# Attention plus conditioned feed-forward on one core: every second unit's two weight addends go to TensorE, products two units behind, rings of six

## The chip, the cores and the metric

One core of one Trainium2 chip runs the whole program. The metric is device time in microseconds (us), the median of several executions. TensorE (PE) multiplies, VectorE (DVE), ScalarE (ACT) and GpSimd (POOL) do element work, SyncE (SP) issues the transfers.

## The reference, cut to what matters

```python
x = x + attn(cond(x, ids, W, b), w_qkv, w_out, slopes)        # x: (2, 2048, 512) fp32
x = x + ffn_int8(cond2(x, ids2, W1, b1, W2, b2, gamma, beta), w8, w8_scale, bias)
# attn, 16 heads of 32:
scores = q @ k.T * scale + alibi;  scores = where(causal, NEG, scores)
num = 0.5 * (1.0 + scores * rsqrt(1.0 + scores * scores))
out = (num / (num.sum(-1) + EPS)) @ v
# cond: x @ W[id] + b[id].   cond2: layer norm of (x + relu(x @ W1 + b1) @ W2 + b2), times gamma, plus beta
```

The kernel never forms `num` itself. With s a score, y = 1/sqrt(1 + s^2) and g = s*y it holds g^2 + y^2 = 1, so (1+g)^2 + y^2 = 2 (1+g) = 4 num. The weight that multiplies v is therefore the sum of two addends, (1+g)^2 and y^2. The factor 4 drops out against the denominator.

## The kernel before, in words

The main part is eight groups, four for each of two batches; a group is four heads. A group walks 40 **units**: a unit is a chunk `c` of 512 queries against a block `kb` of 128 keys, 4 (c+1) blocks for chunk c, so the chunks have 4, 8, 12 and 16 units. The last four units of a chunk lie on the causal diagonal and are 512, 384, 256 and 128 queries wide. A unit is two **pairs** k = 2u and 2u+1 of two heads; a pair's tile is 128 x 1024 at full width. For each pair, in this order:

- PE writes the scores into one of two PSUM slots (L825; on the diagonal with a mask, L828), once the pair two before has given its slot free;
- ACT squares them into `yb` (L669), then takes 1/sqrt(1 + .) in place (L671): y;
- DVE multiplies scores by y into `gb` (L1042): g, which frees the slot;
- POOL squares y in place (L623); ACT makes (1+g)^2 in place (L661), two pairs later in its queue;
- DVE adds the two (`numerator`, L983), two pairs later;
- PE multiplies the sum with v into `ov` and with ones into `dn` (`products`, L804), four heads side by side in columns of 32. It stands `LAG` = 3 units behind the scores. `ov` and `dn` are one PSUM bank each: when a chunk is finished DVE copies both out (L996, L997; between groups L1078, L1079), and only then may the next chunk's first product start (`s_out`). Six and twelve pairs later come a reciprocal and `divide` (L1007).

Between the scores the PE does **parts** of other jobs: projections of q, k, v (`Group`, a planner that fills PE time after each pair's scores). Groups 1, 2, 5 and 6 are `plain` and have only their 12 projections. `opening` (group 0) and `closing` (group 3) also compute the conditioned input h (jobs `xt`, `h`). `joining` (group 4) and `ending` (group 7) also do the output projection and the adapter with its norm for the finished batch (jobs `o`, `rt`, `a`, `w2`, `zt`), 16 and 10 tiles; each job's PSUM result is emptied by DVE into SBUF, all counted by one semaphore `s_evac`. All engines walk the same list of events of a group, each taking its own part; every queue is in order. Plain groups run in hardware loops of two turns.

Of the kernel before, what the change touches and what calls it, by code (L numbers as in the profile page):

```python
# [7 lines left out]
ALU = mybir.AluOpType  # L8
ACT = mybir.ActivationFunctionType
# [14 lines left out]
NORMED = 2  # L24
STAGED = 3
YRING = 4
GRING = 8
NUM_LAG = 2
LAG = 3
# [51 lines left out]
def woven(jobs_of, tiles, n=2):  # L81

    return number([job for j in tiles[::n] for step in zip(*[jobs_of(j + i) for i in range(n)]) for job in step])


class Group:
# [4 lines left out]
    def __init__(self, n_chunks, others, has_next, opens=False, slack=0.0):  # L91
# [30 lines left out]
        for k in range(2 * len(self.units)):  # L122
# [24 lines left out]
            if k % 2:  # L147
                self.events.append(("pv", k // 2 - LAG))
# [4 lines left out]
        assert len(self.items) % BANKS == 0 or not has_next  # L153
# [10 lines left out]
def adaln_attn_ffn(nc, x, ids_cond, ids_lang, cond_w, cond_b, w_qkv, w_out, slopes, W1, b1, W2, b2,  # L164
# [35 lines left out]
    assert PAIRS % YRING == 0 and PAIRS % GRING == 0  # L200
# [6 lines left out]
    def runs(b):  # L207

        return [(0, opening if b == 0 else joining, 1), (1, plain, NG - 2), (NG - 1, ending if b == B - 1 else closing, 1)]

    starts, n = {}, PRO
    for b in range(B):
        for hg, g, count in runs(b):
            starts[b, hg] = n
            n += count * len(g.items)
    REST = n
    PRO_JOBS = woven(cond_jobs, range(TT))
    END_JOBS = woven(after_jobs, range(DONE, KB), KB - DONE)
    PLACES = 2 + KB - DONE
# [9 lines left out]
    def for_groups(eng, body):  # L229

        for b in range(B):
            for hg0, g, count in runs(b):
                if count == 1:
                    body(b, hg0, b * NG + hg0, g, starts[b, hg0])
                else:
                    with eng.Fori(hg0, hg0 + count) as hg:
                        body(b, hg, b * NG + hg, g, starts[b, hg0] - hg0 * len(g.items) + hg * len(g.items))

    with ExitStack() as ctx:
# [13 lines left out]
        yb = sb("yb", [P, YRING, 2 * CH])  # L253
        gb = sb("gb", [P, GRING, 2 * CH])
# [17 lines left out]
        rstd = sb("rstd", [P, PLACES])  # L272
        amax = sb("amax", [P, B * KB])
# [33 lines left out]
        s_evac = sem("s_evac")  # L307
        s_hi = sem("s_hi")
# [6 lines left out]
        s_g2 = sem("s_g2")  # L315
        s_num = sem("s_num")
# [37 lines left out]
        ring_y = yb[:, :, :].rearrange("p a n -> p (a n)")  # L354
        ring_g = gb[:, :, :].rearrange("p a n -> p (a n)")
# [8 lines left out]
        woT_s = gb[:, 0:2, :].rearrange("p a n -> p (a n)").rearrange("p (m c) -> p m c", m=KC)  # L364
        wqT_s = gb[:, 2:8, :].rearrange("p a n -> p (a n)").rearrange("p (g s k n) -> p g s k n", g=NG, s=3, k=KC)
        w8T_s = area[:, 2 * KC * C:2 * KC * C + KC * C // 2].bitcast(BF16).rearrange("p (m c) -> p m c", m=KC)
        idx = yb[0:64, 0:2, :].rearrange("p a n -> p (a n)").bitcast(I32)

        z0 = gb[:, :, :].rearrange("p (k a) n -> p k (a n)", k=KC)
        x10 = kst[:, :, :].bitcast(F32)  # L370
        zq = yb[:, :, :].rearrange("p a n -> p (a n)").bitcast(BF16).rearrange("p (a k n) -> p a k n", a=4, k=KC)
# [11 lines left out]
        def yview(k):  # L383
            return yb[:, k % YRING, :].rearrange("p (h n) -> p h n", h=2)

        def gview(k):
            return gb[:, k % GRING, :].rearrange("p (h n) -> p h n", h=2)

        def q0_of(g, k):

            return g.width(k // 2 % UNITS)
# [17 lines left out]
        def ops_before(g, G):  # L409

            return 2 if g is opening else 2 * NC * G + 3

        @block.sync
        def _(sp):
# [82 lines left out]
            def after(b, job, i):  # L497
# [4 lines left out]
                if what == "o":  # L502
                    sp.wait_ge(s_evac, i + 1)
# [3 lines left out]
                elif what == "zt":  # L507
# [3 lines left out]
                    sp.wait_ge(s_evac, i + 1)  # L511
                    sp.dma_start((hT if b == B - 1 else z_d)[:, :, tok], resT[a]).then_inc(s_zst[a], 16)

            def group(b, hg, G, g, base):
# [3 lines left out]
                if g in (joining, ending):  # L518
                    d = b if g is ending else b - 1

                    sp.wait_ge(s_evac, base)
# [3 lines left out]
                if g is closing:  # L525
                    sp.wait_ge(s_evac, base)
# [3 lines left out]
                for e in g.events:  # L530
# [9 lines left out]
                    what, c = e[1].name[0:2]  # L540
                    if what in ("q", "k"):
# [599 lines left out]
```

## Time and profile before

| | |
|---|---|
| time, median of 3 (lowest, highest) | 2264.09 us (2263.49, 2267.63) |
| the profiled execution | 2265.64 us, span 2263.8 us |
| mean granted PE clock | 0.907 of full |
| busy: DVE, PE, POOL, ACT | 1878.6, 1803.9, 1715.7, 1685.0 us |
| share of the span: DVE, PE, POOL, ACT | 83%, 80%, 76%, 74% |

Busy is the time in which an engine works on at least one instruction; overlapping ones count once. A PE that is busy at half clock does half as much. The shares are means over eight groups with different limits, so the groups have to be read one by one.

### The profile page before, as it was taken

Reading aid. Unit: us, or ns where it says so; the run is one execution under the profiler, and the core shown is the slowest. Engines: PE = TensorE matmul, PEld = TensorE weight load, DVE = VectorE, ACT = ScalarE, POOL = GpSimd, SP = SyncE. Lnnn points to the kernel's source line nnn. Section 1 sums busy time; section 2 is a strip of 40 time slices with the busy share of each in tenths; the row PEclk is TensorE's granted clock in tenths of the full one; section 3 lists DMA queues with packets and bytes.
Section 4 is the critical chain, followed back from the end, with each engine's and each line's share of the span. In section 5 each row is a group of like instructions: output and inputs, shape, how many; then the busy total and the mean of one; then the engine's idle time right before and its main releaser. Section 6 shows DMA issues by size and latency. Waiting matters only on the chain.

```text
span 2263.8 us, 31228 instructions
## 1 busy us (share of the span) xinstructions
PE 1803.9 (80%) x10640; PEld 904.5 (40%) x10640; DVE 1878.6 (83%) x2114; ACT 1685.0 (74%) x1938; POOL 1715.7 (76%) x784
## 2 busy tenths in 40 slices
PE   5678877877787789998888877877787787887864
PEld 4555323333333346664444433333333333342331
DVE  4358888888889888889789898888888888899768
ACT  0247897989889888889567667999889888767413
POOL 2136887788878887788678887788878887788548
PEclk9899988988898899999999998988988898998879
DMA  5411111110111022202322221110111021121137
GB/s 176 146 49 44 49 30 35 43 45 25 40 40 49 20 69 66 68 25 74 84 77 81 69 54 34 40 49 21 45 40 48 20 79 44 42 62 52 59 123 237
DMA packets 126620, 138.68 MB, mean 61 GB/s; under 512 B 27868, under 2 KB 78044, under 8 KB 126044
## 3 DMA queue, kind: packets, MB, share of 16 engines
q1 hardware_dynamic: 126460, 136.64, 21.5%
q8 instruction: 89, 1.46, 0.3%
q14 instruction: 71, 0.58, 0.1%
HBM read 54.02 MB, written 22.80 MB: 34 GB/s over the span
## 4 chain that ended last, share of the span: by engine, by line
PE 38%; ACT 21%; DVE 20%; issue 12%; POOL 4%; DMA 2%; SPq 2%; DVEq 0%; POOLq 0%; ACTq 0%
ACT yb L669 9%; PE sc L825 7%; PE ov L804 7%; ACT yb L671 7%; DVE gb L1042 6%; PE dn L804 6%; ACT gb L661 6%; DVE gb L983 5%; PE it L723 5%; PE it L740 4%; PE it L747 4%; PE it L727 3%; POOL oT L654 2%; SPq L428 2%; PE it L707 1%
## 5 line engine op out<-in xcount | busy, mean ns | idle before, releaser
L623 POOL TENSOR_TENSOR yb<-yb 128x1024 f32<-128x1024 f32 (+3 forms) x640 | 1510.2, 2373 | 460.9 <-DVE gb L1042 448.6
L669 ACT ACTIVATE yb<-sc 128x1024 f32<-128x1024 f32 (+3 forms) x640 | 566.9, 886 | 376.3 <-PE sc L825 189.8
L1042 DVE TENSOR_TENSOR gb<-sc,yb 128x1024 f32<-128x1024 f32 (+3 forms) x640 | 676.6, 1057 | 186.1 <-ACT yb L671 183.9
L983 DVE TENSOR_TENSOR gb<-gb,yb 128x1024 f32<-128x1024 f32 (+3 forms) x640 | 779.2, 1218 | 3.9 <-ACT gb L661 0.5
L825 PE MATMUL sc<-qmv,kst 128*128 128x512 f32 (+3 forms) x1280 | 505.6, 472 | 295.8 <-DVE gb L1042 278.2
L671 ACT ACTIVATE yb<-yb 128x1024 f32<-128x1024 f32 (+3 forms) x640 | 595.0, 930 | 20.3
L661 ACT ACTIVATE gb<-gb 128x1024 f32<-128x1024 f32 (+3 forms) x640 | 584.1, 913 | 0.1
L825 PEld LDWEIGHTS sc<-qmv,kst 128*128 128x128 f32 x1280 | 238.7, 209 | 648.3 <-DVE gb L1042 453.3
L804 PE MATMUL ov<-gb,vv 128*32 128x512 f32 (+3 forms) x2560 | 338.4, 604 | 18.0 <-DVE den L997 10.5
L804 PE MATMUL dn<-gb,ones 128*32 128x512 f32 (+3 forms) x2560 | 326.3, 584 | 0.0
L723 PE MATMUL it<-hT,wT 128*128 128x512 f32 x496 | 249.9, 629 | 5.8 <-DVE area L921 1.8
L804 PEld LDWEIGHTS dn<-gb,ones 128*32 128x32 f32 x2560 | 90.2, 121 | 181.9 <-issue 176.3
L740 PE MATMUL it<-area 128*128 128x128 f32 x1024 | 131.2, 284 | 19.4 <-DVE area L904 18.3
L740 PEld LDWEIGHTS it<-area 128*128 128x128 f32 x1024 | 126.4, 199 | 26.7 <-DVE area L904 21.8
L723 PEld LDWEIGHTS it<-hT,wT 128*128 128x128 f32 x496 | 97.8, 204 | 82.7 <-issue 66.5
L747 PE MATMUL it<-area,oT 128*128 128x512 f32 x224 | 116.3, 648 | 17.4 <-DVE oT L1007 5.7
L727 PE MATMUL it<-wT,hT 128*128 128x128 f32 x992 | 124.5, 279 | 2.9 <-DVE stage L901 2.3
L727 PEld LDWEIGHTS it<-wT,hT 128*128 128x128 f32 x992 | 121.1, 194 | 8.8 <-DVE stage L901 2.5
L828 PE MATMUL sc<-unseen,ident 128*128 128x128 bf16 x512 | 121.8, 243 | 0.0
L804 PEld LDWEIGHTS ov<-gb,vv 128*32 128x32 f32 x2560 | 52.4, 112 | 133.4 <-issue 82.2
L707 PE MATMUL it<-ident,area 128*128 128x128 f32 x336 | 53.5, 293 | 29.3 <-DMA area<-in_x_dram 13.1
L899 DVE TENSOR_SCALAR stage<-it 128x512 fp32r<-128x512 f32 x64 | 43.7, 683 | 34.7 <-PE it L723 20.8
(112 smaller groups left out, 1093.5 us busy)
## 6 DMA issues: line engine op xcount, KB each, us to landing
qmv<-stage SPq DMA_DIRECT2D x384, 64.0 KB
kst<-stage SPq DMA_DIRECT2D x384, 64.0 KB
area<-in_x_dram SPq DMA_DIRECT2D x58, 256.0 KB, 2.8
out_dram<-oT SPq DMA_DIRECT2D x32, 256.0 KB, 3.3
den<-rec_d SPq DMA_DIRECT2D x31, 256.0 KB
wT<-wT_d SPq DMA_DIRECT2D x7, 768.0 KB, 4.4
x_d<-area SPq DMA_DIRECT2D x16, 256.0 KB, 2.6
z_d<-area SPq DMA_DIRECT2D x16, 256.0 KB, 3.2
```

What stands on the lines that cost most here:

```text
L623: pool.tensor_tensor(y, y, y, ALU.mult).then_inc(s_y2, 1)
L661: act.activation(t, t, ACT.Square, bias=1.0).then_inc(s_g2, 1)
L669: act.activation(y, sc[:, k % SLOTS, :, q0_of(g, k):], ACT.Square).then_inc(s_s2, 1)
L671: act.activation(y, y, ACT.Abs_reciprocal_sqrt, bias=1.0).then_inc(s_y, 1)
L723: r = pe.matmul(bank, wT[:, "qk".index(what), part, :], hT[:, part, c * CH:(c + 1) * CH], **ends)
L727: r = pe.matmul(bank[:, part * P:(part + 1) * P], hT[:, k, tok], wT[:, 2, k, :], start=(k == 0), stop=(k == KC - 1))
L740: r = pe.matmul(bank[:, part * P:(part + 1) * P], wc[:, k, part * P:(part + 1) * P], xT[:, a, k, :], start=(k == 0), stop=(k == KC - 1))
L747: r = pe.matmul(bank, oT[:, part, tok], woT[:, part, :], **ends)
L804: r = pe.matmul(dst[h * D:(h + 1) * D, q0:], lhsT, gview(2 * u + h // 2)[:, h % 2, q0:], start=(kb == 0), stop=last_kb)
L825: r = pe.matmul(slot[:, i, q0:], kst[:, h, kb * P:(kb + 1) * P], qmv[:, c % 2, h, q0:], start=True, stop=not on_diagonal)
L983: dve.tensor_tensor(t, t, yview(k)[:, :, q0:], ALU.add).then_inc(s_num, 1)
L1042: dve.tensor_tensor(gview(k)[:, :, q0:], sc[:, k % SLOTS, :, q0:], yview(k)[:, :, q0:], ALU.mult).then_inc(s_g, 1)
```

## The change

1. Pairs get a kind by their number: `KINDS = ("split", "split", "sum", "sum")`. In even units (both pairs split) DVE makes no sum; PE accumulates (1+g)^2 and y^2 one after the other, 16 products in place of 8. In odd units all stays, with lags of one pair in place of two.
2. `LAG` 3 to 2 units, and the product is placed after the scores of an even pair instead of an odd one. The copy of a finished chunk is put off (`leaving`) until after the next odd pair's g.
3. Rings: y four and g eight tiles before, six and six now.
4. The PSUM results of `rt`, `a` and `zt` are emptied by ACT, with a count of their own (`s_evac_act`); the maximum over z stays on DVE (`largest`). The norm on POOL takes one more small instruction.
5. The loops over plain groups are written out.

```diff
-YRING = 4
-GRING = 8
-NUM_LAG = 2
-LAG = 3
+RING = 6
+KINDS = ("split", "split", "sum", "sum")
+SQUARE_LAG = 1
+SUM_LAG = 1
+LAG = 2
...
-            if k % 2:
+            if k % 2 == 0:
                 self.events.append(("pv", k // 2 - LAG))
...
             def products(G, g, u):
-                pe.wait_ge(s_num, G * PAIRS + 2 * u + 2)
+                n = G * PAIRS + 2 * u
+                for m in (n, n + 1):
+                    if kind(m) == "split":
+                        pe.wait_ge(s_y2, m + 1)
+                        pe.wait_ge(s_g2, squared(m) + 1)
+                    else:
+                        pe.wait_ge(s_num, summed(m) + 1)
                 last_kb = kb == TT * (c + 1) - 1
+                heads = [(h, gview(n + h // 2)[:, h % 2, q0:], True, kind(n + h // 2) != "split") for h in range(HG)]
+                heads += [(h, yview(n + h // 2)[:, h % 2, q0:], False, True) for h in range(HG) if kind(n + h // 2) == "split"]
                 for dst, is_v in ((ov, True), (dn, False)):
-                    for h in range(HG):
+                    for h, weights, begins, ends in heads:
...
                 def scored(k):
                     dve.tensor_tensor(gview(n)[:, :, q0:], sc[:, n % SLOTS, :, q0:], yview(n)[:, :, q0:],
                                       ALU.mult).then_inc(s_g, 1)
-                    if k >= NUM_LAG or carry:
-                        numerator(G, g, k - NUM_LAG)
+                    if n >= SUM_LAG and kind(n - SUM_LAG) != "split":
+                        numerator(n - SUM_LAG)
+                    while reduced and reduced[0][0] < k:
+                        largest(*reduced.pop(0)[1:])
+                    if k % 2 and leaving:
+                        u, c = leaving.pop()
+                        if u >= 0:
+                            output(G, hg, g, u, c, g is opening and c == 0)
+                        else:
+                            output_prev(G, prev_hg, u, c)
...
+            def after(b, job, item, z_before):
+                act.wait_ge(s_item, item + 1)
+                if what == "rt":
+                    act.activation(resT[a], feat, ACT.Copy).then_inc(s_evac_act, 1)
+                elif what == "a":
+                    act.activation(hid[a], bank[:, 0:P], ACT.Relu, bias=b1c[:, 0:1]).then_inc(s_evac_act, 1)
+                elif what == "zt":
+                    for k in range(KC):
+                        r = act.activation(resT[a][:, k, :], feat[:, k], ACT.Identity, scale=gam[:, k:k + 1],
+                                           bias=bet[:, k:k + 1])
```

How the queues stand in a plain group where the products pass from chunk 0 (units 0 to 3) to chunk 1 (from unit 4). On PE before: the scores of pair 14, two parts of a projection, the scores of pair 15, two parts, then the first product of unit 4, which waits for `s_out`.

```order
L825 MATMUL sc<-qmv,kst 128x512 [waits s_g]
L825 MATMUL sc<-qmv,kst 128x512
L833 REGISTER_ALU
L716 REGISTER_ALU [waits s_evac]
L723 MATMUL it<-hT,wT 128x512 [waits s_evac]
L723 MATMUL it<-hT,wT 128x512
L817 REGISTER_ALU
L825 MATMUL sc<-qmv,kst 128x512 [waits s_g]
L825 MATMUL sc<-qmv,kst 128x512
L723 MATMUL it<-hT,wT 128x512 x2
L847 REGISTER_ALU
L804 MATMUL ov<-gb,vv 32x512 [waits s_num,s_evac,s_out]
```

On PE in the changed kernel, the same passage: the last product of chunk 0 (unit 3, width 128), the scores of pair 11, two parts, the scores of pair 12, then unit 4's product.

```order
L902 MATMUL ov<-ring,vv 32x128 [waits s_num]
L902 MATMUL ov<-ring,vv 32x128 x3
L902 MATMUL dn<-ring,ones 32x128 x4
L924 MATMUL sc<-qmv,kst 128x512 [waits s_g]
L924 MATMUL sc<-qmv,kst 128x512
L816 MATMUL it<-hT,wT 128x512 x2
L924 MATMUL sc<-qmv,kst 128x512 [waits s_g]
L924 MATMUL sc<-qmv,kst 128x512
L902 MATMUL ov<-ring,vv 32x512 [waits s_g2,s_y2,s_evac,s_out]
L902 MATMUL ov<-ring,vv 32x512 x7
L902 MATMUL dn<-ring,ones 32x512 x8
L924 MATMUL sc<-qmv,kst 128x512 [waits s_g]
```

Unit 4's product moved from behind pair 15 to behind pair 12, has 16 matmuls in place of 8, and no part stands directly ahead of it any more.

On DVE before, the copy of chunk 0: the division of the chunk before, g of pair 13, a numerator, the copy and the denominator.

```order
L1007 TENSOR_TENSOR oT<-oT,den 128x512 [waits s_out]
L1041 REGISTER_ALU [waits s_pv]
L1042 TENSOR_TENSOR gb<-sc,yb 128x1024 [waits s_y]
L983 TENSOR_TENSOR gb<-gb,yb 128x1024 [waits s_g2,s_y2]
L992 REGISTER_ALU
L995 REGISTER_ALU [waits s_pv]
L996 ISA [waits s_norm]
L996 COPY oT<-ov 128x512
L997 TENSOR_SCALAR den<-dn 128x512
```

On DVE in the changed kernel, the same: g of pairs 9 and 10, the division, a projection's two instructions (`stage`), g of pair 11, the numerator of pair 10, the copy and the denominator.

```order
L1147 TENSOR_TENSOR ring<-sc,ring 128x1024 [waits s_y,s_pv] x2
L1109 TENSOR_TENSOR oT<-oT,den 128x512 [waits s_out,s_den]
L1002 TENSOR_SCALAR stage<-it 128x512 [waits s_op,s_qk,s_item]
L1004 SCALAR_TENSOR_TENSOR stage<-it,stage 128x512 [waits s_hi]
L1147 TENSOR_TENSOR ring<-sc,ring 128x1024 [waits s_y,s_pv]
L1085 TENSOR_TENSOR ring<-ring 128x1024 [waits s_g2,s_y2]
L1098 COPY oT<-ov 128x512 [waits s_norm,s_pv]
L1099 TENSOR_SCALAR den<-dn 128x512
```

The copy moved from behind g of pair 13 to behind g of pair 11, two pairs, while the product that waits for it moved three pairs.

## Rows read from the trace of the kernel before

**Rows 1.** Busy time by stretch; rows are groups 0, 1, 3, 4, 5, 7 and the tail
```profile
core 0: us, PE busy (x) PEld busy (x) DVE busy (x) ACT busy (x) POOL busy (x), PEclk, DMA share, GB/s
90.40:371.90 281.50, 227.56 (x1471) 131.73 (x1471) 209.62 (x215) 207.54 (x240) 190.36 (x80) 0.92 0.16 42
371.90:604.30 232.40, 181.29 (x1057) 79.56 (x1057) 198.74 (x197) 205.44 (x240) 191.86 (x81) 0.89 0.15 37
...
836.20:1075.60 239.40, 223.09 (x1633) 139.24 (x1632) 215.87 (x229) 206.80 (x241) 192.32 (x81) 0.99 0.21 59
1075.60:1392.60 317.00, 269.37 (x1473) 133.77 (x1472) 282.79 (x389) 209.74 (x241) 249.79 (x129) 0.96 0.25 68
1392.60:1624.20 231.60, 180.82 (x1057) 79.43 (x1057) 198.38 (x197) 205.41 (x240) 191.47 (x81) 0.89 0.15 38
...
1856.80:2138.20 281.40, 224.87 (x1220) 105.10 (x1222) 246.43 (x306) 205.89 (x238) 223.34 (x109) 0.88 0.18 49
2138.20:2263.80 125.60, 77.11 (x340) 34.86 (x332) 93.81 (x150) 32.54 (x22) 78.07 (x54) 0.87 0.56 180
```
**Rows 2.** Groups of ACT instructions in plain group 5 (1392.6 to 1624.2)
```profile
L669 ACT ACTIVATE yb<-sc 128x1024 f32<-128x1024 f32 x56 | 56.6, 1011 | 13.7 <-PE sc L825 9.2 <-PE sc L828 2.4 <-DVE gb L983 2.0
...
L671 ACT ACTIVATE yb<-yb 128x256 f32<-128x256 f32 x8 | 3.3, 417 | 0.3
```
**Rows 3.** Timeline where group 5 passes from chunk 0 to 1: start, duration, instruction
```profile
1473.24 1.00 ACT L669 ACTIVATE yb<-sc 128x1024 f32<-128x1024 f32 x1
...
1475.22 2.38 DVE L1007 TENSOR_TENSOR oT<-oT,den 128x512 f32 x1
...
1476.18 1.01 ACT L669 ACTIVATE yb<-sc 128x1024 f32<-128x1024 f32 x1
...
1477.22 1.06 ACT L671 ACTIVATE yb<-yb 128x1024 f32<-128x1024 f32 x1
1477.52 1.21 DVE L1042 TENSOR_TENSOR gb<-sc,yb 128x1024 f32<-128x1024 f32 x1
...
1478.65 1.21 DVE L983 TENSOR_TENSOR gb<-gb,yb 128x1024 f32<-128x1024 f32 x1
...
1479.36 1.88 PE L723 MATMUL it<-hT,wT 128*128 128x512 f32 x4
...
1479.79 0.68 DVE L996 COPY oT<-ov 128x512 f32 x1
...
1480.39 0.68 DVE L997 TENSOR_SCALAR den<-dn 128x512 f32<-128x512 f32 x1
...
1481.16 1.06 PE L804 MATMUL ov<-gb,vv 128*32 128x512 f32 x8
...
1482.05 1.04 PE L804 MATMUL dn<-gb,ones 128*32 128x512 f32 x8
...
1483.02 0.73 PE L825 MATMUL sc<-qmv,kst 128*128 128x512 f32 x2
1483.25 0.68 DVE L899 TENSOR_SCALAR stage<-it 128x512 fp32r<-128x512 f32 x1
...
1483.79 1.02 ACT L669 ACTIVATE yb<-sc 128x1024 f32<-128x1024 f32 x1 [0.75 <-PE sc L825]
1483.96 0.69 DVE L901 SCALAR_TENSOR_TENSOR stage<-it,stage 128x512 fp32r<-128x512 f32 x1
```
**Rows 4.** Timeline of PE in group 5 after a wait, clock granted at half
```profile
1410.55 1.93 PE L804 MATMUL ov<-gb,vv 128*32 128x512 f32 x8 [1.36 <-DVE den L1079]
...
1414.12 1.22 PE L825 MATMUL sc<-qmv,kst 128*128 128x512 f32 x2
```
**Rows 5.** PE's waits in group 7 (1856.8 to 2138.2): total us, times, longest
```profile
PE it L747 <- DVE oT L1007: 5.7, 1, 5.7
PE it L747 <- issue: 5.6, 1, 5.6
```
**Rows 6.** Timeline of DVE in group 7: one `zt` tile emptied
```profile
2014.64 1.36 DVE L930 TENSOR_SCALAR area<-it,gam,bet 128x128 f32<-128x128 f32 x4
```

More of the change, by code:

```diff
@@ L207, in runs @@
     def runs(b):
-        return [(0, opening if b == 0 else joining, 1), (1, plain, NG - 2), (NG - 1, ending if b == B - 1 else closing, 1)]
-    starts, n = {}, PRO
+        return ([(0, opening if b == 0 else joining)] + [(hg, plain) for hg in range(1, NG - 1)] +
+                [(NG - 1, ending if b == B - 1 else closing)])
+    starts, n = {}, (PRO, PRO, 0)
     for b in range(B):
-        for hg, g, count in runs(b):
+        for hg, g in runs(b):
             starts[b, hg] = n
-            n += count * len(g.items)
-    REST = n
+            n = tuple(v + w for v, w in zip(n, (len(g.items), g.evacs["dve"], g.evacs["act"])))
+    REST, REST_DVE, REST_ACT = n
     PRO_JOBS = woven(cond_jobs, range(TT))
     END_JOBS = woven(after_jobs, range(DONE, KB), KB - DONE)
+    END_ITEMS = [job for job in END_JOBS if job.parts]
+    END_RANKS, END_EVACS = ranks(END_ITEMS)
     PLACES = 2 + KB - DONE
@@ L227, in tiles_in, with for_groups @@
         return 1 if a >= 2 else (B * KB - (KB - DONE)) // 2
-    def for_groups(eng, body):
+    def for_groups(body):
         for b in range(B):
[L232 to L237, printed above, removed]
+            for hg, g in runs(b):
+                body(b, hg, b * NG + hg, g, starts[b, hg])
     with ExitStack() as ctx:
@@ L381, in adaln_attn_ffn, with kind, before, summed @@
         wq_t = w_qkv.rearrange("(s m p) c -> p s m c", s=3, p=P)
[L383 to L391, printed above, removed]
+        def kind(n):
+            return KINDS[n % len(KINDS)]
+        def before(n, *kinds):
+            count = [k in kinds for k in KINDS]
+            return n // len(KINDS) * sum(count) + sum(count[:n % len(KINDS)])
+        def summed(n):
+            return before(n, "fold", "sum")
+        def squared(n):
+            return before(n, "split", "sum")
+        def yview(n):
+            return ring[:, n % RING, :].rearrange("p (h n) -> p h n", h=2)
+        def gview(n):
+            return ring[:, RING + n % RING, :].rearrange("p (h n) -> p h n", h=2)
+        def q0_of(n):
+            return plain.width(n % PAIRS // 2)
         def div_steps(g, carry):
@@ L411, in ops_before, with zs_before @@
             return 2 if g is opening else 2 * NC * G + 3
+        def zs_before(b, j):
+            order = [job.name[1] for job in (ending if b == B - 1 else joining).items if job.name[0] == "zt"]
+            n = KB * b
+            return n + (order.index(j - 2) + 1 if j >= 2 else 0)
         @block.sync
@@ L553, in group @@
                     elif what in ("o", "zt"):
-                        after(b if g is ending else b - 1, e[1], base + item)
+                        after(b if g is ending else b - 1, e[1], base + item, (act_base if what == "zt" else dve_base) + rank)
                     item += 1
-            for_groups(sp, group)
+            for_groups(group)
             sp.wait_ge(s_pv, B * NG * UNITS)
@@ L675, in _ @@
             act.wait_ge(s_chain, 9)
             act.wait_ge(s_wst, 48)
[L677 to L679 removed]
+            for_groups(group)
+            for n in range(TOTAL - SQUARE_LAG, TOTAL):
+                if kind(n) != "fold":
+                    one_plus_g_squared(n)
+            for job, (eng, rank) in zip(END_ITEMS, END_RANKS):
+                if eng == "act":
+                    after(B - 1, job, REST + job.index, 0)
@@ L1079, in output_prev @@
                 dve.tensor_scalar(den[:, :], dn[:, :], SOFT_EPS, None, ALU.add).then_inc(s_out, 1)
-            for_groups(dve, group)
-            for k in range(-NUM_LAG, 0):
-                numerator(B * NG, plain, k)
+            for_groups(group)
+            for n in range(TOTAL - SUM_LAG, TOTAL):
+                if kind(n) != "split":
+                    numerator(n)
             output_prev(B * NG, NG - 1, -1, NC - 1)
```

273 lines of the change are left out of this document (165 added, 108 removed).

## The prediction

> **What bounds the kernel now.** DVE is the busiest engine of the whole, but the stages differ, so I cut the span where ACT squares the first pair of each group and read the busy times of each stretch [rows 1]. The reader is to see three kinds. A plain group takes 231.6 us and ACT works 205.4 of them, PE 180.8, DVE 198.4: ACT is the nearest to a limit. At full width its three passes over a pair come round in 2.94 us when nothing holds them (1473.24 to 1476.18) [rows 3]; its 26.2 us of idle time stand mostly before L669, for scores that PE brings late [rows 2]. In closing PE works 223.1 of 239.4 us at a clock of 0.99: PE bounds it. In joining DVE works 282.8 of 317.0 and PE 269.4: both. Opening and ending are mixtures, with PE at 227.6 of 281.5 and 224.9 of 281.4 [rows 1]. So a change that takes work from DVE and gives it to PE helps joining at best, and has to be paid in closing.
>
> **What is added to PE.** One product at full width and full clock takes from 1481.16 to 1483.02, 1.86 us: 0.89 for `ov`, 0.97 for `dn` with what lies before the next scores [rows 3]. The added addend repeats both: the doubled product takes 1.78 + 1.86 = 3.64 us. Of a group's 20 even units 16 are full and 4 are 256 wide; counting those as half, 18 x 1.78 = 32 us of PE time for each group. Less per group is not possible, as the four column groups are already used side by side.
>
> **What is taken from DVE.** In the half of the pairs that are split the L983 addition goes, 1.21 us each [rows 3], 36 full-width equivalents or 43 us a group. In joining DVE also loses 16 x (0.68 + 0.34 + 1.36) for `rt`, `a`, `zt`; the 1.36 is [rows 6], the 0.68 the COPY of [rows 3], 0.34 is a quarter of the 1.36. That is 38 us more: 283 falls to about 202. DVE stops being a limit anywhere. ACT gets those jobs: not less than 1.9 us a tile if it does them at its own speed per element, not more than 0.6 + 0.4 + 4 x 0.42 = 2.7 us if each 128-wide piece costs what 256 columns cost it [rows 2]. 16 tiles are 30 to 43 us on 209.7, far below the 301 us that PE needs there, so I cost it at nothing; if that cover were gone it would be those 30 to 43.
>
> **What moves: the passage from chunk to chunk.** This is the term I give most weight. `ov` and `dn` are single, so the next chunk's first product waits for DVE's copy. Before, that product stands behind the scores of pair 15, which themselves wait for g of pair 13, and the copy follows g of 13 and one numerator: the two come together, and ACT loses only 0.75 us (the row at 1483.79) [rows 3]. Now the product stands behind the scores of pair 12, which need only g of pair 10, while the copy stands behind g of 11 and the numerator of 10. Let T be the start of ACT's square of pair 11. g(11) starts at T + 2.08 (1.01 + 1.06 for the two passes); from the start of g to the start of the product rows 3 give 1481.16 - 1477.52 = 3.64 us (g, sum, copy, denominator). So the product starts at T + 5.72. It is unit 4, an even one, and doubled: the scores of pair 13 start at T + 9.36, ACT's square 0.77 later (1483.02 to 1483.79), at T + 10.13. ACT wanted it at T + 5.88. It stands still for 4.2 us. All four first units of a chunk (0, 4, 12, 24) are even, so all four passages have this form. In two of them a division and a projection's two evacuations stand ahead of that g: the division would start at T + 0.27 and, with 2.30 to the next (1475.22 to 1477.52) and 0.68 + 0.69, puts g at about T + 3.9 instead of T + 2.08: 6.0 us. The passage between groups, at narrow pairs, I take as the mean of these three, 5.4. Together 21.6 us for a group with nothing else in PE's queue there. The PE idles for some 5 us in each.
>
> **The plain group.** Floor 205.4; passages 21.6. Doubled products also follow two projection parts at four places: from the end of g, 0.09 + 0.57 for scores, 1.8 for parts, 3.64, 0.77 are 6.9 us against the 5.5 that ACT allows, 1.3 each; three more stand at 256-wide pairs, about 1 each: 8 us. A rest of 1. The clock: after a wait of 1.36 us in [rows 4] the granted clock was at half, and one product took 1410.55 to 1414.12, 3.57 instead of 1.86 us. The mean clock of plain groups is 0.89 now [rows 1]; more PE work between the passages raises it, the 5 us of idle time in each lowers it. A whole doubled product at half clock costs 3.6 us more, so the four passages give 0 to 14; I take 5, nearer the low end, as the clock comes back during the product. Sum 241, which is **+9 each, +36 for four** (bounds 214 and 250: -68 to +73).
>
> The Trainium skill, page "TensorE: Matmul & The Clock Gate", section "HAM oscillation", says that an idle stretch of waiting sends the array back to the slow clock, so that the next burst starts cold each time. By that rule each passage would cost its whole doubled product, 14 in place of 5, and the sum would be 36 us higher; this is the second rival.
>
> **The other groups.** Closing: 223.1 + 32 = 255 busy, and of its 16.3 us of PE idle time 9 stay, since two parts stand ahead of most first products and fill 1.8 of each wait: 264, **+25** (+16 if none stays, +32 if all). Joining: 269.4 + 32 = 301, and of 47.6 us of PE idle time, mostly for DVE, a third stays: 317, **0** (-15 to +20). The passages there are covered by two or three parts. Ending: 224.9 + 32 = 257, the two waits for a division that remain 11.3 [rows 5], passages 5.4 + 6.0 and, where parts help, 2 x 2.5: 285, **+3** (-15 to +15). Opening: one bare passage 4.2, one half filled 2.4, some of the rest: **+8** (0 to +28). Tail: six tiles' `rt`, `a`, `zt`, up to 6 x 2.38 = 14 us of DVE time, go beside it on ACT; DVE was busy 93.8 of 125.6 [rows 1]: **-5** (0 to -14). The written-out loops save some register instructions of plain groups between waits, and the rings of six add no wait, since the product they wait for stands ahead of the scores in PE's queue: nothing for both.
>
> **Sum.** 36 + 25 + 0 + 3 + 8 - 5 = +67 on the profiled execution's 2265.6: 2333. That execution lies 1.5 above the median of the three, so 2331.
>
> **Rivals.**
> - *The relief of DVE wins (faster), 0.22.* For it: DVE is the busiest engine, and every g in joining waits behind evacuations; ACT's idle time in plain groups could shrink as g comes sooner. Against it: [rows 3] show that g is on time when ACT is. It needs the passages to be short, because parts or an earlier copy cover them: then plain groups 222 (-40), closing +18, joining -12, ending -12, opening +4, tail -7: -49, 2215. With the other groups as forecast it decides where passages and clock together cost a plain group less than 9.5 of the 26.6 us that I gave them (plain groups at 224, 4 x -7.75 = -31).
> - *The clock falls at each passage (slower still), 0.12.* Plain groups 250, ending and opening 5 more each: about 2375 to 2400.
> - *ACT becomes late through evacuations, 0.03.* Its queue is in order, so `rt` or `zt` may hold back squares; joining and ending +10 and +5: 2346. PE's need of 301 us in joining speaks against it.
> - *Gains and costs cancel, 0.07*: within 0.2%, which is about what a measurement of this kernel tells from no change.
>
> **How the numbers follow.** My forecast has 0.56. Slower by over 0.2% is 0.56 + 0.12 + 0.03 = 0.71, same 0.07, faster 0.22. Cases of both signs count, so the range goes from just under the faster rival, 2210, to the clock rival's end, 2400; the forecast's own range is 2285 to 2370.
>
> **What would show it.** In the changed profile: waits of `ov` at the copy (PE behind L1099) of several us, 16 in plain groups; `ov` and `dn` busy time up by some 250 us; DVE near 1450 us busy, ACT near 1750; closing above 255 us; plain groups near 241, with ACT idle in lumps of 4 to 6 us right after first products. It is wrong if plain groups come under 228 or if those waits stay under 1 us; if closing is under 250, the product's price is wrong.

## The result, and the profile after

The changed kernel takes 2470.8 us (median of 4, 2467.61 to 2472.82) against 2265.86 for the kernel before on the same chip: 1.0902 times as long, interval 1.0881 to 1.0923. I had said 2331, 67 us slower; it is 205 us slower. The profiled execution has a span of 2466.8 us and a mean granted clock of 0.927.

Busy times went where the sum had put them. DVE fell to 1419.2 us and ACT rose to 1753.9 (I had about 1450 and 1750). `ov` and `dn` together took 338.4 + 326.3 us before; together they now take 272 more (I had 250). In these rows an fp32 product matmul of the program stands as two records:

```profile
L902 PE MATMUL ov<-ring,vv 128*32 128x512 f32 (+3 forms) x3840 | 488.7, 616 | 161.3 <-DVE den L1099 76.9 <-DVE ring L1085 62.9 <-DVE den L1198 21.4
L902 PE MATMUL dn<-ring,ones 128*32 128x512 f32 (+3 forms) x3840 | 448.3, 569 | 0.0
```

The idle time did not. The stretches of the changed kernel, cut as in [rows 1] at ACT's first square of each group; the rows are groups 0 to 7 and the tail, the columns those of [rows 1]:

```profile
90.40:387.30 296.90, 253.80 (x1791) 141.45 (x1791) 161.67 (x175) 208.13 (x241) 155.02 (x79) 0.95 0.15 39
387.30:645.20 257.90, 206.70 (x1378) 87.27 (x1377) 148.55 (x157) 205.30 (x241) 156.60 (x80) 0.91 0.13 34
645.20:904.60 259.40, 208.22 (x1378) 87.90 (x1377) 148.52 (x157) 205.36 (x241) 156.60 (x80) 0.91 0.15 40
904.60:1180.40 275.80, 257.38 (x1954) 150.57 (x1953) 168.94 (x189) 206.70 (x241) 155.55 (x80) 0.98 0.19 54
1180.40:1528.30 347.90, 302.93 (x1794) 146.82 (x1793) 205.01 (x253) 243.61 (x337) 198.60 (x144) 0.95 0.22 60
1528.30:1788.60 260.30, 209.62 (x1378) 88.26 (x1377) 148.58 (x157) 205.33 (x241) 156.59 (x80) 0.90 0.13 33
1788.60:2048.00 259.40, 208.21 (x1378) 87.79 (x1377) 148.50 (x157) 205.33 (x241) 156.62 (x80) 0.91 0.16 43
2048.00:2343.40 295.40, 246.79 (x1548) 112.06 (x1550) 173.59 (x208) 226.44 (x298) 183.55 (x120) 0.94 0.16 43
2343.40:2466.80 123.40, 77.18 (x329) 34.98 (x328) 78.18 (x111) 46.35 (x56) 70.63 (x58) 0.86 0.58 183
```

Every group is longer. Set against [rows 1], a plain group grew by 27 us, and in it PE's busy time by 25 to 29, so that PE still idles for some 51 us of it. Joining grew by 31, PE's busy time by 33.6, though DVE, which [rows 1] show as the busiest engine of joining, gave up 78 us there. PE's idle time in joining was 47.6 us before and is 45.0 now, but not the same time. Before, 45.9 us of its waits ended on DVE and none on ACT; now 22.8 end on DVE and 20.3 on ACT, which empties the tiles of `rt`, `a` and `zt`. The longest waits of the two profiles in joining, before first; each line has the waiting engine, its work and line, the releaser; us in total, times, the longest:

```profile
PE sc L825 <- DVE gb L1042: 13.8, 9, 2.7
PE it L756 <- DVE area L918: 11.6, 8, 3.1
PE it L707 <- DVE stage L901: 7.7, 4, 3.2
...
PE it L800 <- DVE stage L1004: 10.7, 3, 3.8
PE sc L924 <- DVE ring L1147: 7.5, 4, 3.5
PE it L849 <- ACT area L722: 6.2, 6, 1.3
PE it L816 <- ACT area L725: 4.5, 1, 4.5
```

Over the whole kernel the list of waits names these releasers for PE's scores and products, in the same columns:

```profile
PE sc L924 <- DVE ring L1147: 132.5, 104, 5.0
PE ov L902 <- DVE den L1099: 76.9, 20, 4.7
PE ov L902 <- DVE ring L1085: 62.9, 39, 3.6
PE ov L902 <- DVE den L1198: 21.4, 7, 3.9
```

The two `den` rows are products that wait for a copied chunk. The row with L1085 is one I had not named at all: products of odd units that wait for the numerator.

**A passage from chunk to chunk**, of the form drawn in the prediction: the timeline of group 5 where chunk 1 passes to chunk 2, with start, duration, instruction and the idle time before it. (ACT has squared pair 28 by then, so this is unit 12. [rows 3], headed chunk 0 to 1, show this same passage of the kernel before: 32 squares of the group stand before the product at 1481.16. The order of the queues is the one drawn.)

```profile
1617.28 0.68 DVE L1099 TENSOR_SCALAR den<-dn 128x512 f32<-128x512 f32 x1
...
1618.01 3.64 PE L902 MATMUL ov<-ring,vv 128*32 128x512 f32 x16 [4.65 <-DVE den L1099]
...
1621.43 2.94 PE L902 MATMUL dn<-ring,ones 128*32 128x512 f32 x16
...
1624.30 1.19 PE L924 MATMUL sc<-qmv,kst 128*128 128x512 f32 x4
...
1625.13 1.02 ACT L746 ACTIVATE ring<-sc 128x1024 f32<-128x1024 f32 x1 [7.04 <-PE sc L924]
```

PE waits 4.65 us for the copy, and then the doubled product takes 6.29 us to the next scores (1618.01 to 1624.30). The granted clock, 1.00 at its upper level and 0.50 at its lower, has a mean of 0.56 from 1618.0 to 1624.3. At a clock of 1.00, 28 us later, the doubled product takes 3.57 (1645.52 to 1649.09); I had 3.64:

```profile
1645.52 1.92 PE L902 MATMUL ov<-ring,vv 128*32 128x512 f32 x16
...
1647.26 1.90 PE L902 MATMUL dn<-ring,ones 128*32 128x512 f32 x16
...
1649.09 0.73 PE L924 MATMUL sc<-qmv,kst 128*128 128x512 f32 x2
```

The Trainium skill, page "TensorE: Matmul & The Clock Gate", section "HAM oscillation — how this bites in real kernels", tells of a kernel whose long waits for data throttle the array again each time, so that the burst behind each of them starts cold. The trace agrees for the four passages of group 5, with waits of 3.41, 4.66, 4.65 and 4.54 us: their doubled products take 6.33, 5.59, 6.29 and 6.18 us in place of 3.57.

**What I had not seen.** Later in the same group the product of an odd unit is late:

```profile
1738.53 4.66 POOL L668 TENSOR_TENSOR ring<-ring 128x1024 f32<-128x1024 f32 x2 [2.42 <-DVE ring L1147]
...
1741.37 2.90 DVE L1085 TENSOR_TENSOR ring<-ring 128x1024 f32<-128x1024 f32 x1 [0.65 <-POOL ring L668]
...
1744.41 1.93 PE L902 MATMUL ov<-ring,vv 128*32 128x512 f32 x8 [2.91 <-DVE ring L1085]
...
1747.98 2.03 PE L924 MATMUL sc<-qmv,kst 128*128 128x512 f32 x4
...
1749.30 1.02 ACT L746 ACTIVATE ring<-sc 128x1024 f32<-128x1024 f32 x1 [2.63 <-PE sc L924]
```

With sums one pair behind g instead of two, the numerator waits for POOL's square of the same pair, starts just as POOL begins the next square, and takes 2.90 us instead of the 1.21 of [rows 3]. In the whole profile all 18 full-width numerators that start less than 0.2 us after a square of POOL take 2.90 us, and all 168 that start ahead of the square take 1.21 to 1.23. The product right behind it waits 2.91, the granted clock is 0.50 from 1744.4 to 1748.0, and ACT stands still for 2.63. The Trainium skill, page "SBUF — State Buffer", section "Who interferes with whom", says that a VectorE instruction with two SBUF inputs contends with GpSimd over a shared port pair, and that issue order decides who blocks. The rows agree: the numerator has two such inputs and takes 2.90; g (L1147), which takes scores from PSUM and one input from SBUF, took 1.22 us beside a running square:

```profile
1615.71 2.80 POOL L668 TENSOR_TENSOR ring<-ring 128x1024 f32<-128x1024 f32 x1 [0.79 <-DVE ring L1147]
...
1617.88 1.22 DVE L1147 TENSOR_TENSOR ring<-sc,ring 128x1024 f32<-128x1024 f32 x1
```

### The profile page after: what moved, and what is told of

Same layout as the page of the kernel before. It is cut to its first block, busy times and chain, and to the rows that moved or that the text cites. A ratio compares the mean times of both kernels' runs of the same rounds, so it can differ in the third digit from the quotient of the medians.

```text
span 2466.8 us, 35012 instructions
## 1 busy us (share of the span) xinstructions
PE 2020.1 (82%) x13197; PEld 975.8 (40%) x13200; DVE 1419.2 (58%) x1602; ACT 1753.9 (71%) x2130; POOL 1406.5 (57%) x816
## 4 chain that ended last, share of the span: by engine, by line
PE 52%; ACT 19%; DVE 14%; issue 7%; POOL 6%; DMA 1%; SPq 1%; DVEq 0%; POOLq 0%; ACTq 0%
PE ov L902 13%; PE dn L902 10%; ACT ring L746 8%; PE sc L924 8%; ACT ring L748 6%; PE it L816 5%; ACT ring L707 4%; PE it L820 4%; DVE ring L1147 4%; DVE ring L1085 4%; PE it L833 3%; POOL ring L668 3%; PE it L840 3%; POOL oT L700 2%; PE it L800 1%
## 5 line engine op out<-in xcount | busy, mean ns | idle before, releaser
L668 POOL TENSOR_TENSOR ring<-ring 128x1024 f32<-128x1024 f32 (+3 forms) x640 | 1236.7, 1938 | 935.7 <-DVE ring L1147 928.5
L1147 DVE TENSOR_TENSOR ring<-sc,ring 128x1024 f32<-128x1024 f32 (+3 forms) x640 | 679.5, 1062 | 661.9 <-ACT ring L748 653.3
L746 ACT ACTIVATE ring<-sc 128x1024 f32<-128x1024 f32 (+3 forms) x640 | 566.8, 886 | 509.2 <-PE sc L924 301.1
L902 PE MATMUL ov<-ring,vv 128*32 128x512 f32 (+3 forms) x3840 | 488.7, 616 | 161.3 <-DVE den L1099 76.9
L748 ACT ACTIVATE ring<-ring 128x1024 f32<-128x1024 f32 (+3 forms) x640 | 594.9, 930 | 20.3
L924 PE MATMUL sc<-qmv,kst 128*128 128x512 f32 (+3 forms) x1280 | 472.7, 450 | 146.1 <-DVE ring L1147 132.5
L707 ACT ACTIVATE ring<-ring 128x1024 f32<-128x1024 f32 (+3 forms) x640 | 584.3, 913 | 10.2 <-DVE ring L1147 10.1
L902 PE MATMUL dn<-ring,ones 128*32 128x512 f32 (+3 forms) x3840 | 448.3, 569 | 0.0
L1085 DVE TENSOR_TENSOR ring<-ring 128x1024 f32<-128x1024 f32 (+2 forms) x320 | 376.7, 1177 | 27.6 <-POOL ring L668 27.5
L902 PEld LDWEIGHTS ov<-ring,vv 128*32 128x32 f32 x3840 | 99.5, 115 | 377.7 <-issue 172.1
L902 PEld LDWEIGHTS dn<-ring,ones 128*32 128x32 f32 x3840 | 134.5, 118 | 273.4 <-issue 262.4
```

The costliest lines, as they stand in the source:

```text
L668: pool.tensor_tensor(y, y, y, ALU.mult).then_inc(s_y2, 1)
L707: act.activation(t, t, ACT.Square, bias=1.0).then_inc(s_g2, 1)
L746: act.activation(y, sc[:, n % SLOTS, :, q0_of(n):], ACT.Square).then_inc(s_s2, 1)
L748: act.activation(y, y, ACT.Abs_reciprocal_sqrt, bias=1.0).then_inc(s_y, 1)
L902: r = pe.matmul(dst[h * D:(h + 1) * D, q0:], lhsT, weights, start=(kb == 0 and begins), stop=(last_kb and ends))
L924: r = pe.matmul(slot[:, i, q0:], kst[:, h, kb * P:(kb + 1) * P], qmv[:, c % 2, h, q0:], start=True, stop=not on_diagonal)
```

## The experiments

The duration of each kernel's groups, from ACT's first squares of each profiled execution (us; "plain" is the mean of four; PE idle is the joining group's length less PE's busy time). The column "time" and the times in the texts below are medians, so they can differ by some us from the profiled execution whose groups stand beside them (by 10 for lags of two).

| kernel | time | ratio | opening | plain | closing | joining | ending | PE idle, joining |
|---|---|---|---|---|---|---|---|---|
| before | 2264 to 2266 | 1 | 281.5 | 232.1 | 239.4 | 317.0 | 281.4 | 47.6 |
| changed | 2470.8 | 1.090 | 296.9 | 259.3 | 275.8 | 347.9 | 295.4 | 45.0 |
| all sums | 2524.1 | 1.114 | 300.7 | 272.5 | 281.0 | 333.4 | 300.6 | 56.8 |
| odd units split | 2419.4 | 1.067 | 298.2 | 251.4 | 270.6 | 334.6 | 298.2 | 40.9 |
| copy at once | 2360.4 | 1.041 | 288.9 | 242.6 | 262.4 | 345.0 | 281.8 | 43.4 |
| one addend | 2340.9 | 1.033 | 287.0 | 246.3 | 249.6 | 322.6 | 281.7 | 47.9 |
| product later | 2402.3 | 1.062 | 294.0 | 248.2 | 256.1 | 347.9 | 292.6 | 42.7 |
| lags of two | 2342.5 | 1.035 | 289.3 | 238.2 | 254.5 | 335.2 | 285.3 | 36.3 |
| lags of two, all sums | 2288.6 | 1.011 | 276.3 | 234.9 | 242.6 | 322.9 | 290.9 | 45.2 |
| lags of two, odd split | 2383.6 | 1.053 | 285.5 | 250.3 | 263.2 | 331.9 | 287.6 | 33.6 |
| three units | 2255.1 | 0.996 | 278.5 | 231.3 | 239.7 | 309.8 | 286.8 | 42.1 |
| warm | 2438.9 | 1.076 | 295.9 | 251.9 | 276.9 | 347.3 | 295.7 | 44.9 |
| lags of two, one addend | 2168.1 | 0.958 | 274.6 | 219.4 | 229.0 | 313.4 | 258.1 | 38.2 |

### The split taken back: all sums, and odd units split

```diff
-KINDS = ("split", "split", "sum", "sum")
+KINDS = ("sum", "sum", "sum", "sum")       # all sums
+KINDS = ("sum", "sum", "split", "split")   # odd units split
```

> The changed kernel with every pair of the kind sum: eight matmuls a product everywhere and a numerator on VectorE for every pair; lags, rings, the late copy and ScalarE's evacuations stay. Theory M (the added matmuls of 256 us are what costs): nearly all of the 205 us comes back, 2265 to 2290. Theory P (the passages from chunk to chunk cost, by the late copy of ov and dn, and the doubled first product is only a part of it): each passage keeps its wait of about 4.6 us and loses 1.8 to 3.5 of the product; the time stays at 2320 to 2370.

> The changed kernel with the odd units split instead of the even ones: the first product of a chunk has eight matmuls again and no numerator stands ahead of the copy; added matmul time is 16 instead of 18 full products a group, about the same. Theory M: -3.6 us a group, 2440 to 2450. Theory P: each passage loses 1.8 of product, 1.1 of numerator and some time at half clock: some 4 us x 4 x 8 where ScalarE is the limit, less where TensorE is; 2350 to 2390.

All sums: 2524.14 us, 1.1141 [1.1118, 1.1164], 53 us *above* the changed kernel, so both theories fell. With everything else as changed, the split helps. The groups of instructions of all sums show where it loses; columns as in [rows 2]:

```profile
L1085 DVE TENSOR_TENSOR ring<-ring 128x1024 f32<-128x1024 f32 (+3 forms) x640 | 903.9, 1412 | 113.0 <-POOL ring L668 110.4
L902 PE MATMUL ov<-ring,vv 128*32 128x512 f32 (+3 forms) x2560 | 368.3, 651 | 339.1 <-DVE ring L1085 194.7 <-DVE den L1099 113.3 <-DVE den L1198 30.7
```

Every numerator is now one pair behind g: DVE waits 110 us for POOL, the mean numerator is 1412 ns (1218 before), and PE's wait for it is 195 us. Odd units split: 2419.36, 1.0673 [1.0653, 1.0693], between the two theories. A single product stands at the passages, which leave ACT idle for 3.8 to 5.1 us in group 5 instead of 6.3 to 7.7.

### The copy at once

```diff
-                            leaving.append((u, c))
+                            if u >= 0:
+                                output(G, hg, g, u, c, g is opening and c == 0)
+                            else:
+                                output_prev(G, prev_hg, u, c)
```

> The changed kernel, with the copy of a finished chunk put right behind its last product in VectorE's queue (after g of an even pair) instead of behind the next odd pair's g and numerator. Theory P: the wait of ov for den, 76.9 us in 20 places, falls below 15 us; plain groups from 259 to about 238, the whole to 2340 to 2375. Theory M: the waits only move into other waits, under 40 us gained, 2430 or more.

2360.43, 1.0413 [1.0382, 1.0445]: 110 us of the 205 are gone. The wait for `den` at L1099 fell from 76.9 to 13.7 us. The wait for the numerator did not:

```profile
PE ov L902 <- DVE ring L1085: 86.8, 54, 3.6
...
PE ov L902 <- DVE den L1099: 13.7, 14, 1.3
```

A passage gone sooner brings the next numerator under POOL's square: its mean rose from 1177 to 1324 ns, and a plain group won 16.7 us of the 28 that ACT had idled at its passages.

### One addend left out

This kernel leaves the y² addend out of the even units, so half of their matmuls are gone and its output is not the reference's.

```diff
-                heads += [(h, yview(n + h // 2)[:, h % 2, q0:], False, True) for h in range(HG) if kind(n + h // 2) == "split"]
```

(The first addend then ends the accumulation as well as beginning it.)

> The changed kernel with the second addend left out of the products of even units (part of the computation is missing: y squared is not added there): eight matmuls everywhere, no numerator in even units, the late copy stays. This is the price of the added matmuls alone. Theory M: 256 us of TensorE time go and all of it shows, 2215 to 2240. Theory P: the four waits of a group of some 4.6 us stay, as in the run with all pairs of the kind sum, 2290 to 2340.

2340.85, 1.0326 [1.0306, 1.0345], 1 us above the range of theory P and far from that of theory M. The added matmuls cost 130 us in the changed kernel; the other 75 are not the split's matmuls.

### Product one pair later, then lags of two

On top of the copy at once; first the products go behind an odd pair's scores, as before, then the two lags of one pair become two.

```diff
-            if k % 2 == 0:
+            if k % 2:
                 self.events.append(("pv", k // 2 - LAG))
...
-SQUARE_LAG = 1
-SUM_LAG = 1
+SQUARE_LAG = 2
+SUM_LAG = 2
```

> The run e3 (copy at once), and each product placed one pair later, behind the scores of an odd pair as in the kernel before. Theory N, formed from the trace of the changed kernel: what is left beside the passages is the numerator of odd units. It stands one pair behind g in VectorE's queue, so it waits for GpSimd's square of the same pair and then runs against GpSimd's next square (2.90 us instead of 1.22), and the product that needs it is next in TensorE's queue. With the product a pair later its wait for L1085, 62.9 us in 39 places, nearly goes; plain groups from 242 to 228 to 233, the whole from 2360 to 2290 to 2320. Theory M (the doubled products themselves are what is left): the work is the same, 2345 or more.

> As e5, and numerator and ScalarE's second square two pairs behind g, as before. Theory N: the numerators of odd units fall back from their mean of 1.18 over all widths to about 1.15 and wait for GpSimd no more (27.5 us to under 3); another 5 to 20 us less than e5. Theory M: same as e5 within 10 us. Either way closing stays near 255 and joining above 320, as TensorE has 32 us more to do in each.

The first: 2402.34, 1.0618 [1.0593, 1.0643], 42 us worse than copy at once. The wait for the numerator did vanish (0.5 us), so the mechanism was real; but the time came back elsewhere. Where chunk 0 passes to chunk 1 in group 5, PE waits 2.31 us for g, does 0.73 us of scores, waits 1.60 for `den`, and then does the doubled product at a mean clock of 0.57, 6.18 us to the scores. ACT idles for 4.0 us there, against 0.9 at the same passage of copy at once, whose wait for `den` is 1.26 us with the clock at 1.00. That this is all of the 42 us is not shown; closing even came out 6 us shorter. PE's timeline, product later:

```profile
1518.76 0.73 PE L925 MATMUL sc<-qmv,kst 128*128 128x512 f32 x2 [2.31 <-DVE ring L1148]
...
1521.09 3.64 PE L903 MATMUL ov<-ring,vv 128*32 128x512 f32 x16 [1.60 <-DVE den L1100]
1524.50 2.84 PE L903 MATMUL dn<-ring,ones 128*32 128x512 f32 x16
1527.27 0.73 PE L925 MATMUL sc<-qmv,kst 128*128 128x512 f32 x2
```

The second: 2342.46, 1.0354 [1.0329, 1.0379], 60 us better than the first, where I had expected 5 to 20. DVE no longer waits for POOL before a numerator, and the mean numerator is 1054 ns instead of the 1108 of product later. From the groups of instructions and the windows (groups 5, 4, 3) of lags of two:

```profile
L1086 DVE TENSOR_TENSOR ring<-ring 128x1024 f32<-128x1024 f32 (+2 forms) x320 | 337.3, 1054 | 2.7 <-ACT ring L708 0.4
```

```profile
1446.50:1686.00 239.50, 205.66 (x1377) 87.24 (x1376) 143.05 (x156) 204.88 (x240) 161.40 (x80) 0.93 0.14 36
1111.20:1446.50 335.30, 299.05 (x1793) 146.97 (x1793) 201.95 (x252) 242.75 (x337) 205.59 (x145) 0.96 0.23 62
856.80:1111.20 254.40, 249.82 (x1953) 149.59 (x1952) 162.30 (x188) 206.65 (x240) 160.86 (x80) 1.00 0.21 58
```

Closing has PE busy for 249.8 of 254.4 us at full clock: that is the limit that the doubled products set there. Which part of the 60 us is the lag of the squares and which that of the sums, no run tells.

### The split at lags of two

```diff
-KINDS = ("split", "split", "sum", "sum")
+KINDS = ("sum", "sum", "sum", "sum")       # all sums
+KINDS = ("sum", "sum", "split", "split")   # odd split
```

> As e6 with every pair of the kind sum, so no added matmuls and a numerator for every pair: all that then differs from the kernel before is the distance of two units, rings of six and ScalarE's evacuations. Theory M: the split costs 25 to 32 us of TensorE in closing and joining each, so this is 40 to 80 us faster than e6, near the kernel before, 2240 to 2270. If instead the relief of VectorE pays for the added matmuls, e6 and e7 are within 15 us of each other.

> As e6 with the odd units split instead of the even ones: 16 instead of 18 added full products a group (3.6 us of TensorE less), and the first product of a chunk single. With the copy at once the passages no longer matter: 10 to 30 us less than e6 by theory M, 0 to 10 less by theory N.

All sums: 2288.61, 1.0114 [1.0092, 1.0136]; the split costs 54 us here, the reverse of its sign at lags of one. Odd split: 2383.6, 1.053 [1.0505, 1.0554], 41 us worse than the even one, where I had expected no worse. The profiles show where the 41 us stand, with 16 instead of 18 added products a group: PE waits 42.9 us before `ov` against 16.3, and 207.7 us for g before scores against 181.8, at a mean clock of 0.925 against 0.944. Why the parity counts for so much, and the other way round than with the late copy and lags of one, stays open.

### Three units behind, four and eight tiles

On top of lags of two with all sums; the waits for a free tile follow the rings. What is left of the change is then the evacuations on ACT, the small instruction more in the norm and the written-out loops.

```diff
-LAG = 2
+LAG = 3
...
-            return ring[:, n % RING, :].rearrange("p (h n) -> p h n", h=2)
+            return ring[:, n % 4, :].rearrange("p (h n) -> p h n", h=2)
...
-            return ring[:, RING + n % RING, :].rearrange("p (h n) -> p h n", h=2)
+            return ring[:, 4 + n % 8, :].rearrange("p (h n) -> p h n", h=2)
```

> The run e7 (all pairs of the kind sum, lags of two pairs, copy at once) with products three units behind and rings of four and eight, as in the kernel before. What then differs from the kernel before is ScalarE's share of the evacuations, the small instruction more in the norm and the written-out loops. If the distance of two units is what keeps e7 24 us above the kernel before, this lies at or below the kernel before: joining, where VectorE was busy 283 of 317 us, falls to 300 to 312, the whole 2240 to 2262. If the evacuations on ScalarE cost (its queue is in order and holds back squares), joining stays at 320 or more and the whole at 2270 to 2290.

2255.05, 0.9964 [0.995, 0.9977], about 8 to 10 us faster than the kernel before and the best of those that compute everything. Its windows (groups 5, 4, 3):

```profile
1379.60:1611.50 231.90, 182.46 (x1057) 79.44 (x1056) 198.28 (x197) 205.09 (x241) 191.33 (x81) 0.88 0.14 37
1069.70:1379.60 309.90, 267.82 (x1473) 133.63 (x1473) 252.06 (x293) 242.99 (x337) 237.91 (x145) 0.97 0.26 71
830.00:1069.70 239.70, 223.15 (x1633) 139.24 (x1632) 216.02 (x229) 206.82 (x240) 192.11 (x81) 0.99 0.21 58
```

Plain and closing are as in [rows 1]; joining is 7 us shorter, with 252.1 us of work on DVE instead of 282.8. Of PE's waits in joining 30.5 us end on DVE (45.9 before) and 10.7 on ACT (none before). The third unit of distance and the rings together are worth 34 us.

### PE kept warm in the passages

The changed kernel with 16 unused matmuls ahead of the first product of each chunk in plain groups; nothing reads what they write.

```diff
+                            if g is plain:
+                                emptied(item - BANKS, g.ranks, dve_base, act_base)
+                                for _ in range(16):
+                                    pe.matmul(it[:, (PRO + item) % BANKS, 0:P], ident[:, :], ident[:, :], start=True, stop=True)
```

> The changed kernel, with 16 small matmuls (ident with ident, about 3.5 us, into an empty bank, their result unused) ahead of the wait for the copy at each passage of the four plain groups, so that TensorE does not stand idle there. Theory C (the doubled first product is slow because the granted clock fell during the wait): product and scores after it take 3.6 instead of 5 to 6.3 us, some 2 us less in each of the 16 passages, plain groups 259 to about 251, the whole 2430 to 2445. If the clock is not the cause, nothing or a few us more: 2470 to 2480.

2438.89, 1.0763 [1.0749, 1.0778], 32 us below the changed kernel, and 7.4 of them in each plain group. PE's timeline at the passage from chunk 1 to 2 of group 5:

```profile
1597.67 3.73 PE L949 MATMUL it<-ident 128*128 128x128 f32 x32
1602.48 1.92 PE L902 MATMUL ov<-ring,vv 128*32 128x512 f32 x16 [1.08 <-DVE den L1103]
1604.22 1.90 PE L902 MATMUL dn<-ring,ones 128*32 128x512 f32 x16
1606.06 1.20 PE L924 MATMUL sc<-qmv,kst 128*128 128x512 f32 x4
```

The copy comes no sooner (4.81 us from the end of the scores to the product, 4.65 in the changed kernel), but the product takes 3.58 us instead of 6.29, and ACT idles for 4.33 instead of 7.04.

### Lags of two with one addend left out

The y² addend is left out of the even units of lags of two, by the edit of "one addend" above.

> This is the kernel with value products one pair later and lags of two (2342 us), with the y-squared addend left out of the even units' products, so that half of the added matmuls are gone and the output is not the reference's. Its time read against 2342 prices the added matmuls, and read against the same lags with every weight summed on VectorE (2289 us) it prices the relief of VectorE alone. Theory R (the relief is worth something once the lags are long, and the matmuls eat it): 2235 to 2275, under 2280, numerator mean near 1050 ns. Theory Z (relief is worth nothing at these lags, the split is pure cost): 2285 to 2300, the whole 54 us being the matmuls. Theory O (the harm of the split is its order, products of two kinds alternating, more than its matmuls): above 2305.

2168.07, 0.9577 [0.9547, 0.9608], below every theory. The added matmuls cost 174 us at lags of two, and relief of DVE without them would win 121 against all sums. Its windows (groups 5, 4, 3):

```profile
1344.90:1566.90 222.00, 179.55 (x1057) 79.48 (x1056) 143.26 (x156) 204.65 (x241) 161.35 (x80) 0.90 0.15 39
1031.50:1344.90 313.40, 275.18 (x1473) 139.92 (x1473) 201.66 (x252) 242.50 (x337) 204.68 (x144) 0.93 0.24 66
802.50:1031.50 229.00, 222.22 (x1633) 139.81 (x1632) 162.26 (x188) 206.13 (x240) 160.82 (x80) 0.99 0.23 65
```

In a plain group the matmuls add 26 us of busy time (179.6 to 205.7) and 17.5 of length (222.0 to 239.5), though in the longer one PE idles for 34 us and ACT for 35. The doubled product stands between two scores; that its length reaches ACT where something else stands there too is argued from the queue, not tried by itself.

## Why the prediction was wrong in size

Of the 205 us, taking the change back in the order of the experiments: the late copy 110 (2471 to 2360), product place and lags of one 18 (to 2342), the split 54 (to 2289), distance and rings 34 (to 2255), evacuations and loops −10. The order counts: at lags of one the split by itself *wins* 53 (2524 to 2471), at lags of two it loses 54. The difference to my sum, by groups: my groups were 241 plain, 264 closing, 317 joining, 285 ending, 289.5 opening; they missed by 73 in the four plain ones, by 12, 31, 10 and 7 us in the others, and the tail by 3, together 136. All misses are on the same side.

- **Product's price: right.** 3.57 against 3.64 us clean; 272 against 250 us of busy time, which products at half clock would explain.
- **Passages: right together, wrong in their parts.** I had 21.6 + 5 for the clock = 26.6 a plain group. ACT's idle times at the four passages of group 5 are 7.7, 6.3, 7.0, 6.8 = 27.9. But the warm run shows that the clock alone is 7.4 of it, not 5: I wrote that "the clock comes back during the product", and at all four the mean granted clock of the product was only 0.55 to 0.67. The rival "the clock falls at each passage" was the true mechanism, at half the price that I gave it. That the sum of the two came out so near is in part luck.
- **Doubled products "8 us" and "a rest of 1": the step that failed in plain groups.** I built a plain group up from ACT's 205.4 us of work and let the 26.2 us that ACT idles in it before [rows 1] go, with 1 us for the rest. One of these is 4.62 us long and stands at the passage between groups (the product of [rows 4], at half clock), so the 0.75 us of [rows 3] was no measure of all four passages before. Of ACT's 55.0 us of idle time in group 5 of the changed kernel, 27.1 are outside the passages. Behind doubled products are seven waits of 1.0 to 1.8 us and one of 2.2, 12.3 together (I had 8). The rest is 14.8 (I had 1): three waits of 2.0 to 2.6 behind late numerators, 7.2, one of which is shown above; 5.0 in pieces under 1 us; 2.6 before ACT's other instructions. I looked only at what waits for a copy and never asked what the lag of one pair does to the sum of the *odd* units, which now needs POOL's square of the pair just done; but that is 7 us of this group's miss of 19, not all of it.
- **Joining: the step "a third stays" failed.** I took two thirds of PE's 47.6 us of idle time as waiting for DVE that would go. Half of the waiting for DVE did go, 45.9 to 22.8 us, as DVE was relieved by 78 us. But I put the evacuations on ACT at nothing, and 20.3 us of waits for ACT's tiles stand in its place. PE's busy time rose by 33.6 as priced, and 45.0 us of idle time stayed. Ending is alike: 15.7 us of PE's waits end on ACT there (none before), 31.9 on DVE (46.3 before); I had said 3 longer, it is 14. In the last column of the table the idle time of joining is 34 to 57 us in every kernel, with DVE at 202 to 283, and the 57 are those of all sums. No run leaves the evacuations on DVE with the rest as changed, so what they cost is read from the waits, not tried. Opening (8, it is 15) and closing (25, it is 36) fell short too. In closing PE idles for 18.4 us, where I had left 9: 16.3 before, and the waits are now for copies (9.7) and numerators (4.7).
- **Evacuations on ACT: right for ACT, wrong for PE.** ACT's busy time in joining is 243.6, inside 209.7 + 30 to 43 (2.1 us a tile), and its squares wait for PE, so the rival "ACT becomes late" did not come in the form that I gave it. What I left out is that PE waits for the tiles (above). On balance the evacuations cost nothing only in the three-units kernel, which has them and the written-out loops and is about 10 us faster than before: joining 7, opening 3, the tail 3, the four plain groups together 3, ending 5 the other way.
- **Rings of six add no wait: nearly so by the trace, not tested alone.** In the changed kernel ACT's squares wait 3.8 us in all for a numerator to free their tile (38.1 before), and g waits 5.7 us in all for a product to free its tile. The three-units kernel changes rings and distance together, for 34 us. I had said nothing for rings and had not priced the distance of two apart from the passages.
- **Relief of DVE wins.** Its point of decision was where passages and clock cost a plain group under 9.5 us. They cost 27.9. The relief itself was underrated, though: without its matmuls it is worth 121 us at lags of two, and at lags of one it is worth more than the matmuls cost, by 53 us. That this is because half of the numerators are gone that meet POOL is argued from the waits, not tried by itself.

## What to carry to other kernels

Time freed on the busiest engine counts only where the trace shows a wait that ends on it, and work handed to another engine brings waits that end on that one: here half of the waits for VectorE went and nearly as much waiting for ScalarE came. When a stage is added up from the busy time of its limiting engine, the idle time that it has already must be carried over, wait by wait, unless the change takes away its cause. When a lag between producer and consumer is shortened, price each consumer again, those that the change isn't about too: here a sum one pair nearer to its input met the other engine's next instruction and took more than twice as long. A late copy costs the wait and, if TensorE's granted clock falls in it, part of the next burst at half clock as well.

## What the runs showed of the hardware

- One and the same 128 x 1024 addition on DVE takes 1.22 us when it starts ahead of POOL's square, which then takes 2.80 (1615.71) instead of 1.89 (1741.30), and 2.90 when it starts just behind the start of the square, which then takes 1.89; the product behind it waits 2.91. With the two lags alone changed, from product later to lags of two, the mean over the same 320 additions falls from 1108 to 1054 ns, and DVE's waits for POOL before them from 22.5 us to none. With all sums it is 1412 ns at lags of one and 1197 at lags of two, where copy and product stand elsewhere too.
- In the product-later run waits of 2.31 and 1.60 us with 0.73 us of scores between them were followed by a doubled product at a mean granted clock of 0.57 (6.18 us); one of 1.08 us behind 3.73 us of unused matmuls by one at a clock of 1.00 (3.58).
- Unused matmuls in the queue made the kernel faster, by 32 us, with the copy no sooner.
